# Layer 1: nearest prototypes from the products, distances on ScalarE, and an fp32 bias product

## The chip, the cores and the metric

One core of one Trainium2 chip runs the whole program in one launch. The metric is the device time of a run in microseconds (us). TensorE (PE) multiplies, VectorE (DVE), ScalarE (ACT) and GpSimd (POOL) do the elementwise work, SyncE (SP) issues most of the DMAs.

## The reference

Two layers, each a cross attention and an FFN, each added to x through a tanh gate, over 64 batches of 256 tokens of 256 values. Layer 0's FFN is a mixture of experts over the first 1024 tokens. The change lies in layer 1's FFN:

```python
def _L1_ffn_ref(x, prototypes, B, A, bias, temp):
    x2 = jnp.sum(xf * xf, axis=1, keepdims=True)
    p2 = jnp.sum(prototypes * prototypes, axis=1)
    d2 = x2 + p2[None, :] - 2.0 * (xf @ prototypes.T)
    dists = jnp.sqrt(jnp.maximum(d2, 0.0))
    t = jnp.maximum(jnp.abs(temp), 0.1)
    w = jax.nn.softmax(-dists / t, axis=1)
    topw, topi = jax.lax.top_k(w, 2)
    topw = topw / jnp.sum(topw, axis=1, keepdims=True)
    ...
        h = jnp.einsum('nri,ni->nr', B[idx], xf)
        y = jnp.einsum('nor,nr->no', A[idx], h) + bias[idx]
        out = out + wt * y
```

There are 32 prototypes with factors of rank 16, so 512 low values a token. Each token takes its two nearest prototypes. x2 is the same for all 32, so the order of the distances is that of the products 2 x p - p2.

## The kernel before

The program runs five phases one after the other: keys and values, layer 0's attention, the experts, and `attention_ffn_phase`, which holds layer 1's attention and FFN in one software pipeline over 64 batches i of two tiles (h = 0 and 1) of 128 tokens; t = 2 i + h counts tiles. Between the experts and layer 1 `Layer1Weights` splits the weights into fp16 halves.

Each engine runs its own `body(i, u, j)` in order, written out for 16 batches and looped over; the engines meet at semaphores (`need(engine, semaphore, value)` is a wait). There is no scheduler: the order on an engine is the order of the code. A body works on several tiles at once, by lag: in the body of tile t the scores of t are made, tile t-3 goes through the transposition of its probabilities (three groups, each split into `probT` hi by ScalarE, L1234, and lo by VectorE, L1492) and its output product, t-4 is normalised, t-5 gets its low products and the products with the prototypes (`dots`), t-6 its two weights, t-7 the weighing and the transposition of the selection, t-8 the up product with its bias, and the residual. In between stand the queries of the next batch, four banks of twelve products, one (the second of h=1's `prep`) at the very end of h=1.

TensorE's results go through a ring of five PSUM banks in a fixed order of uses. A bank is written only when its earlier use has been read; the second low bank of h=0 follows the first probT bank, the output bank the third. So a late `probT_lo` on VectorE stops TensorE there.

What the change touches, for tile t:

- VectorE, `prototype_products` (L1531): dots = scale times product minus |p|^2. `nearest_two` (L1540, L1544): near = min(dots - |y|^2, -tiny), then MAX8 of near. `nearest_index` (L1549): the places. A `hold` is a wait followed by a small memset.
- GpSimd, `top_weights`: dist = -top (L1179), index to float (L1180), root by a power (L1182), the difference, decay to its power (L1184), plus one (L1185). Behind it stand `weighed_low` (L1171, for which SP's transposition of hw waits) and others.
- VectorE, `pick` (L1627, twice) = (iota == index) * weight, and `wsel` (L1634) = the sum of both, written three times side by side, 96 columns. GpSimd's `weigh` (L1192) multiplies the 512 low values by it.
- TensorE transposes wsel (L1468, fp32). ScalarE evacuates 96 rows as fp16 (L1353), VectorE takes the third block's rounding off (L1608), so that wselT holds hi, hi and lo. The bias, held as hi, lo, hi, is one fp16 product over 96 rows (L1452), the last of tile t-8's bank.
- ScalarE, `length2` (L1282): |y|^2 of tile t-4, in one of two columns of `ysq`.

## Time and profile before

| | us |
|---|---|
| median of 3 runs | 3045.66 |
| lowest and highest | 3040.59, 3046.47 |
| the profiled execution | 3044.48 |
| its span, first to last instruction | 3042.80 |
| TensorE busy in it | 2739.6 (90%) |
| VectorE busy | 2507.4 (82%) |
| GpSimd busy | 2089.8 (69%) |
| ScalarE busy | 1983.7 (65%) |

Busy time counts what an engine executes; a matmul's record is longer than its share of the array, since matmuls overlap, so the distance between starts says what one costs. "h=0" and "h=1" below are the halves of a batch by TensorE's body; VectorE runs ahead, so the end of its own body of h=1 (`a_wsel`, `a_near`) falls into the stretch in which TensorE is in h=0. A line of the chain of waits is a piece of the path that ended last, followed back from the end.

### The profile page before, as it was taken

How to read it: one execution, taken by the hardware profiler on the slowest of the kernel's cores; microseconds unless marked ns; L12 is line 12 of the kernel's file. 1: busy time of each engine (PE TensorE's matmuls, PEld its weight loads, DVE VectorE, ACT ScalarE, POOL GpSimd, SP SyncE). 2: the span in 40 equal slices, each digit the busy share in tenths (PEclk: the TensorE clock that was granted, in tenths of full speed). 3: DMA queues.
4: the chain of work that ended last, by engine and by line, in shares of the span. 5: the costliest groups of instructions: out<-in, count | busy, mean ns of one | idle time of the engine just before them, and what ended most of it. 6: DMA issues, size and time to landing. Idle time of an engine off the chain costs nothing.

```text
span 3042.8 us, 96434 instructions
## 1 busy us (share of the span) xinstructions
PE 2739.6 (90%) x31534; PEld 2166.8 (71%) x31534; DVE 2507.4 (82%) x6126; ACT 1983.7 (65%) x4683; POOL 2089.8 (69%) x2777
## 2 busy tenths in 40 slices
PE   4888896899999999689699999999989999999996
PEld 2444444677777777557578888888878888888885
DVE  6877776688888888675689999899989989999885
ACT  2666666687777877575466666666656666666663
POOL 3893000567666676544388888888888888888886
PEclk9999998899999999899899999999999999999998
DMA  5987566223233232631567766666776767766663
GB/s 152 364 337 294 235 254 256 76 81 93 77 90 84 80 93 76 220 117 41 121 142 158 158 147 149 140 145 150 145 137 149 141 144 149 147 150 145 145 132 78
DMA packets 638943, 455.55 MB, mean 150 GB/s; under 512 B 389760, under 2 KB 612592, under 8 KB 633648
## 3 DMA queue, kind: packets, MB, share of 16 engines
q1 hardware_dynamic: 618288, 402.31, 52.2%
q0 software_dynamic: 7328, 23.40, 2.5%
q10 hardware_dynamic: 12960, 25.23, 2.2%
q8 instruction: 195, 3.19, 0.5%
q14 instruction: 172, 1.41, 0.2%
HBM read 235.08 MB, written 148.83 MB: 126 GB/s over the span
## 4 chain that ended last, share of the span: by engine, by line
PE 32%; DVE 6%; issue 4%; POOL 3%; SPq 2%; ACT 2%; DMA 1%; DVEq 0%; POOLq 0%; ACTq 0%
PE banks L150 10%; PE banks L152 9%; PE banks L151 9%; PE banks L1416 2%; DVE a_near L1540 2%; PE banks L1401 2%; SPq L1058 1%; DVE a_probT_lo L1492 1%; ACT a_qT_hi L1234 1%; DVE a_pick L1627 1%; DVE a_rsum L1504 1%; DVE a_wtop L1567 1%; POOL a_pn L1154 1%; DMA a_xnT<-a_xn_parts 0%; DMA a_hwT<-a_hw_parts 0%
## 5 line engine op out<-in xcount | busy, mean ns | idle before, releaser
L1234 ACT ACTIVATE a_qT_hi<-banks 128x512 f16<-128x512 f32 x252 | 150.4, 597 | 540.8 <-PE banks L152 540.8
L383 POOL TENSOR_TENSOR a_probT_lo<-a_expT,a_probT_hi 128x512 f16<-128x512 f32 x256 | 291.4, 1159 | 218.5 <-ACT a_probT_hi L466 218.5
L459 ACT ACTIVATE a_expT<-banks,a_top,w_score_scale 128x512 f32<-128x512 f32 (+1 forms) x384 | 272.4, 709 | 152.5 <-PE banks L550 146.1
L1154 POOL TENSOR_TENSOR a_pn<-a_prob,a_rsum 128x1024 f32<-128x1024 f32 (+1 forms) x256 | 310.2, 1233 | 5.8 <-DVE a_rsum L1506 5.8
L150 PE MATMUL banks<-a_xnT,w_q_hi 128*128 128x256 f16 x1024 | 281.2, 275 | 15.0 <-DMA a_xnT<-a_xn_parts 13.2
L150 PE MATMUL banks<-a_vo_front,a_probT_hi 128*128 128x256 f16 x1024 | 279.8, 273 | 9.4 <-DVE a_probT_lo L1492 6.5
L152 PE MATMUL banks<-a_xnT,w_q_lo 128*128 128x256 f16 x1024 | 280.6, 274 | 0.0
L151 PE MATMUL banks<-a_xnT,w_q_hi 128*128 128x256 f16 x1024 | 280.6, 274 | 0.0
L152 PE MATMUL banks<-a_vo_front,a_probT_lo 128*128 128x256 f16 x1024 | 279.7, 273 | 0.0
L151 PE MATMUL banks<-a_vo_front,a_probT_hi 128*128 128x256 f16 x1024 | 279.6, 273 | 0.0
L1490 DVE TENSOR_TENSOR a_qT_lo<-banks,a_qT_hi 128x512 f16<-128x512 f32 x252 | 172.0, 683 | 77.9 <-ACT a_qT_hi L1234 77.7
L1234 ACT ACTIVATE a_probT_hi<-banks 128x512 f16<-128x512 f32 (+1 forms) x384 | 197.8, 515 | 22.4 <-PE banks L1416 18.0
L1492 DVE SCALAR_TENSOR_TENSOR a_probT_lo<-banks,a_probT_hi 128x512 f16<-128x512 f32 (+1 forms) x384 | 207.2, 580 | 3.5 <-ACT a_probT_hi L1234 3.5
L550 PE MATMUL banks<-ident,a_shifted 128*128 128x128 f32 (+1 forms) x1280 | 204.2, 283 | 5.3
L2366 DVE SCALAR_TENSOR_TENSOR kv_vo_out<-banks,kv_vo_out 128x512 f16<-128x512 f32 (+1 forms) x312 | 191.4, 677 | 19.2 <-ACT kv_vo_out L2264 19.2
L1416 PE MATMUL banks<-ident,a_pn 128*128 128x128 f32 (+1 forms) x1280 | 197.3, 277 | 5.5 <-POOL a_pn L1154 3.6
L659 DVE TENSOR_TENSOR a_shifted<-banks,a_smax 128x1024 f32<-128x1024 f32 (+1 forms) x256 | 192.1, 792 | 3.8
L2264 ACT ACTIVATE kv_vo_out<-banks 128x512 f16<-128x512 f32 (+1 forms) x312 | 172.1, 602 | 30.8 <-DMA vo<-kv_vo_out 24.2
L1171 POOL TENSOR_TENSOR a_hw_parts<-a_hw,a_hw_parts 128x512 f16<-128x512 f32 x128 | 148.0, 1156 | 59.7 <-ACT a_hw_parts L1307 59.7
L649 DVE TENSOR_REDUCE a_smax<-banks 128x16 f32<-128x1232 f32 x128 | 183.5, 1434 | 2.4 <-PE banks L536 1.9
L1192 POOL TENSOR_TENSOR a_hw<-a_low,a_wsel 128x512 f32<-128x512 f32 x128 | 135.2, 1056 | 59.3 <-DVE a_wsel L1634 59.3
L1143 POOL TENSOR_TENSOR a_half<-a_prob 128x512 f32<-128x512 f32 x128 | 165.7, 1295 | 14.3 <-ACT a_prob L1324 14.3
(380 smaller groups left out, 10177.7 us busy)
## 6 DMA issues: line engine op xcount, KB each, us to landing
vo<-kv_vo_out SPq DMA_DIRECT2D x38, 2048.0 KB, 8.1
a_vo_front<-vo SPq DMA_DIRECT2D x128, 512.0 KB
kt<-kv_k_out ACTq DMA_DIRECT2D x9, 2560.0 KB, 14.9
a_k<-kt SPq DMA_DIRECT2D x64, 308.0 KB, 3.5
kv_raw_e<-in_L_ffn_w POOLq DMA_DIRECT2D x16, 1024.0 KB, 8.9
a_x<-in_x SPq DMA_DIRECT2D x64, 256.0 KB, 2.9
a_y<-in_x SPq DMA_DIRECT2D x64, 256.0 KB, 2.7
x<-a_y SPq DMA_DIRECT2D x64, 256.0 KB, 2.8
```

The lines of the kernel that those rows point to most:

```text
L150: nc.tensor.matmul(out, lhs[0], rhs[0], start=start, stop=False)
L151: nc.tensor.matmul(out, lhs[0], rhs[1], start=False, stop=False)
L152: return nc.tensor.matmul(out, lhs[1], rhs[0], start=False, stop=stop)
L383: pool.tensor_tensor(probT[b][1][:, first:end, :], expT[b][:, first:end, :], probT[b][0][:, first:end, :], ALU.subtract).then_inc(prob_rea ...
L459: act.activation(expT[1 - h][0:rows, first:end, :], bank, ACT.Exp, bias=top[0:rows, 0:1], scale=weights["score_scale"][0:rows, 0:1]).then_ ...
L550: last = nc.tensor.transpose(bank[0:rows, c * P:(c + 1) * P], shifted[1 - h][:, place:place + rows], ident[:, :])
L659: last = nc.vector.tensor_tensor(shifted[h][:, cols].rearrange("p (r h k) -> p r h k", r=TILES, k=end - first), held_scores[:, :, :, first ...
L1154: last = pool.tensor_tensor(keys_of(pn[h]), e[:, :, first:end], rsum[h][:, :].unsqueeze(2).broadcast_to([P, H, end - first]), ALU.mult)
L1234: act.activation(out, bank[:, 0:cols].rearrange("p (c s) -> p c s", c=out.shape[1]), ACT.Copy, scale=scale)\
L1416: last = nc.tensor.transpose(bank[0:rows, c * P:(c + 1) * P], pn[1 - h][:, place:place + rows], ident[:, :])
L1492: nc.vector.scalar_tensor_tensor(out=lo, in0=bank, scalar=scale, in1=hi, op0=ALU.mult, op1=ALU.subtract)\
L2366: nc.vector.scalar_tensor_tensor(out=vo_out[q][0:m, placed(b), 1, :], in0=product_banks(g, c, b, m), scalar=1.0 / OUT_TOP, in1=vo_out[q][0 ...
```

## The change

Three things. (1) The maximum and its index are sought in `dots` itself; `near` is gone, and with it the subtraction of |y|^2 before. (2) The squared distances of the two found come from ScalarE, `square_gaps`: Relu(|y|^2 - top), put in ScalarE's body one tile later, behind the first probT_hi (and, in h=1, a query bank), ahead of `norm2_log`. It waits for the maximum and is waited for by `top_weights` on GpSimd, which adds a tiny number in place of the change of sign. `ysq` has four columns. (3) The bias product runs in fp32 over 32 rows: wsel is 32 columns wide and written once, ScalarE's evacuation writes fp32, VectorE's L1608 is gone, and the bias is loaded once and only scaled.

```diff
-            for n, number in enumerate((-0.5, 0.5, -1.0, 1.0)):
+            for n, number in enumerate((-0.5, 0.5, TINY, 1.0)):
...
-    ysq = sb("ysq", [P, TPB])
-    dots, near = sb("dots", [P, NPROTO]), sb("near", [P, NPROTO])
+    ysq = sb("ysq", [P, LENGTHS])
+    dots, idle_top = sb("dots", [P, NPROTO]), sb("idle_top", [P, 1])
     top, topi, topf = sb("top", [P, 8]), sb("topi", [P, 8], U32), sb("topf", [P, 2])
-    dist, dgap, late, wtop = sb("dist", [P, 2]), sb("dgap", [P, 1]), sb("late", [P, 1]), sb("wtop", [P, 2])
+    dist, square, dgap, late, wtop = sb("dist", [P, 2]), sb("square", [P, 2]), sb("dgap", [P, 1]), sb("late", [P, 1]), sb("wtop", [P, 2])
     more, euler, decay = sb("more", [P, 1]), sb("euler", [P, 1]), sb("decay", [P, 1])
     pick = sb("pick", [P, 2, NPROTO])
-    wsel = sb("wsel", [P, P])
-    wselT = sb("wselT", [BIAS_ROWS, P], F16)
+    wsel = sb("wsel", [P, NPROTO])
+    wselT = sb("wselT", [NPROTO, P])
...
-            need(pool, top_used, t)
-            pool.tensor_tensor(dist[:, :], top[:, 0:2], numbers[:, 2:3].broadcast_to([P, 2]), ALU.mult).then_inc(top_used, 1)
+            need(pool, gap_ready, t + 1)
+            kept = pool.tensor_tensor(dist[:, :], square[:, :], numbers[:, 2:3].broadcast_to([P, 2]), ALU.add)
             pool.tensor_copy(topf[:, :], topi[:, 0:2]).then_inc(top_ready, 1)
-            need(pool, top_used, t + 1)
+            step(kept)
             step(pool.tensor_tensor(dist[:, :], dist[:, :], numbers[:, 1:2].broadcast_to([P, 2]), ALU.pow))
...
+        def square_gaps(t, h, u):
+
+            n = (TPB * u + h - 6) % LENGTHS
+            need(act, top_found, t + 1)
+            need(act, ysq_done, t + 1)
+            need(act, more_ready, t)
+            act.activation(square[:, :], top[:, 0:2], ACT.Relu, bias=ysq[:, n:n + 1], scale=-1.0).then_inc(gap_ready, 1)
...
-        def length2(t, h):
-
+        def length2(t, h, u):
+
+            n = (TPB * u + h - 4) % LENGTHS
             need(act, ln2_inverse, t + 1)
-            need(act, near_ready, t - 1)
-            act.activation(ysq[:, h:h + 1], inv2[:, :], ACT.Identity, scale=mv2[:, 1:2]).then_inc(ysq_done, 1)
+            act.activation(ysq[:, n:n + 1], inv2[:, :], ACT.Identity, scale=mv2[:, 1:2]).then_inc(ysq_done, 1)
...
                     if g == 0:
                         prep(0)
+                        if live(t - 6, NT):
+                            square_gaps(t - 6, h, u)
                         if live(t - 4, NT):
...
-                    act.activation(wselT[:, :], bank[0:BIAS_ROWS, 0:P], ACT.Copy).then_inc(wselT_hi, 1)
+                    act.activation(wselT[:, :], bank[0:NPROTO, 0:P], ACT.Copy).then_inc(wselT_ready, 1)
...
-                    filled(nc.tensor.transpose(bank[:, 0:P], wsel[:, :], ident[:, :]), i, ("wselT", h))
+                    filled(nc.tensor.transpose(bank[0:NPROTO, 0:P], wsel[:, :], ident[:, :]), i, ("wselT", h))
...
-            need(dve, near_ready, t)
+            need(dve, topi_found, t)
...
-        def nearest_two(t, h):
-
+        def nearest_two(t):
+
+            need(dve, gap_ready, t)
             need(dve, dots_read, t + 1)
-            need(dve, ysq_done, t + 1)
-            nc.vector.tensor_scalar(near[:, :], dots[:, :], ysq[:, 1 - h:2 - h], -TINY, ALU.subtract, ALU.min)\
-                .then_inc(near_ready, 1)
-            need(dve, top_used, t)
-            hold(near_ready, t + 1)
-            nc.vector.max(top[:, :], near[:, :]).then_inc(top_found, 1)
+            nc.vector.memset(idle_top[:, :], 0.0)
+            nc.vector.max(top[:, :], dots[:, :]).then_inc(top_found, 1)
 
         def nearest_index(t):
 
             hold(top_found, t + 1)
-            nc.vector.max_index(topi[:, :], top[:, :], near[:, :]).then_inc(topi_found, 1)
+            nc.vector.max_index(topi[:, :], top[:, :], dots[:, :]).then_inc(topi_found, 1)
...
-                if live(t - 7, NT):
-                    bank, rows = full(i, ("wselT", h)), slice(2 * NPROTO, BIAS_ROWS)
-                    need(dve, wselT_hi, t - 6)
-                    nc.vector.tensor_tensor(wselT[rows, :], bank[rows, 0:P], wselT[rows, :], ALU.subtract)\
-                        .then_inc(wselT_ready, 1)
...
-                    nc.vector.tensor_tensor(wsel[:, 0:BIAS_ROWS].rearrange("p (r n) -> p r n", r=3),
-                                            pick[:, 0, :].unsqueeze(1).broadcast_to([P, 3, NPROTO]),
-                                            pick[:, 1, :].unsqueeze(1).broadcast_to([P, 3, NPROTO]), ALU.add)\
-                        .then_inc(wsel_ready, 1)
+                    nc.vector.tensor_tensor(wsel[:, :], pick[:, 0, :], pick[:, 1, :], ALU.add).then_inc(wsel_ready, 1)
                 if live(t - 5, NT):
-                    nearest_two(t - 5, h)
+                    nearest_two(t - 5)
...
-        for r in range(3):
-            sp.dma_start(self.raw_bias[r * NPROTO:(r + 1) * NPROTO, :], low_bias).then_inc(self.small_in, 16)
+        sp.dma_start(self.low_bias_sb[:, :], low_bias).then_inc(self.small_in, 16)
...
-        dve, low_bias_sb, raw_bias = self.nc.vector, self.low_bias_sb, self.raw_bias
-        step = Steps(dve, self.bias_step, 0, 1)
-        step(dve.tensor_scalar(raw_bias[:, :], raw_bias[:, :], self.low_unit[0:BIAS_ROWS, 1:2], None, ALU.mult))
-        dve.tensor_copy(low_bias_sb[:, :], raw_bias[:, :]).then_inc(self.bias_hi, 1)
+        dve, low_bias_sb = self.nc.vector, self.low_bias_sb
+        dve.tensor_scalar(low_bias_sb[:, :], low_bias_sb[:, :], self.low_unit[0:NPROTO, 1:2], None, ALU.mult)
         for n, (parts, src, unit) in enumerate(self.turned_jobs):
             split16(self.nc, False, *parts, src, self.inverse[:, unit:unit + 1], self.hi_done, n + 2, self.lo_done)
-        dve.wait_ge(self.bias_hi, 1)
-        rows = slice(NPROTO, 2 * NPROTO)
-        dve.tensor_tensor(low_bias_sb[rows, :], raw_bias[rows, :], low_bias_sb[rows, :], ALU.subtract)
```

On VectorE, at the end of its body of h=1 and the start of the next body, before (a line number, the operation, out<-in):

```order
L1634 TENSOR_TENSOR a_wsel<-a_pick 128x96
L1540 TENSOR_SCALAR a_near<-a_dots,a_ysq 128x32
L847 MEMSET a_idle 128x1
L1544 MAX a_top<-a_near 128x8
L847 MEMSET a_idle 128x1
L1549 MAX_INDEX a_topi<-a_top,a_near 128x8
L62 ISA
L62 REGISTER_ALU
L1504 TENSOR_REDUCE a_rsum<-a_quarter 128x16
```

and now:

```order
L1633 TENSOR_TENSOR a_wsel<-a_pick 128x32
L1547 MEMSET a_idle_top 128x1
L1548 MAX a_top<-a_dots 128x8
L846 MEMSET a_idle 128x1
L1553 MAX_INDEX a_topi<-a_top,a_dots 128x8
L61 ISA
L61 REGISTER_ALU
L1511 TENSOR_REDUCE a_rsum<-a_quarter 128x16
```

`a_near` (L1540) is gone between `a_wsel` and the maximum; a memset of one column that waits for nothing new stands there. Behind follow, as before, the row sums and the splits that TensorE waits for.

On ScalarE, at the start of its body of h=0, behind the next batch's a_xn_parts, before:

```order
L1291 ACTIVATE a_xn_parts<-a_xn 128x2x256
L62 ISA
L1234 ACTIVATE a_probT_hi<-banks 128x512
L62 ISA
L1264 ACTIVATE a_minus_mean<-a_mv 128x1
L1265 ACTIVATE a_vare<-a_mv,eps 128x1
L1234 ACTIVATE a_probT_hi<-banks 128x512
L1324 ACTIVATE a_prob<-a_prob,w_score_scale 128x1232
```

and now:

```order
L1297 ACTIVATE a_xn_parts<-a_xn 128x2x256
L61 ISA
L1232 ACTIVATE a_probT_hi<-banks 128x512
L61 ISA
L61 REGISTER_ALU
L1276 ACTIVATE a_square<-a_top,a_ysq 128x2
L61 REGISTER_ALU
L1262 ACTIVATE a_minus_mean<-a_mv 128x1
L1263 ACTIVATE a_vare<-a_mv,eps 128x1
L1232 ACTIVATE a_probT_hi<-banks 128x512
L1332 ACTIVATE a_prob<-a_prob,w_score_scale 128x1232
```

`a_square` (L1276) has come in ahead of the statistics of the second norm; the exponential and the other pieces of `a_probT_hi` stand behind it. (ISA and REGISTER_ALU rows wait for or compute a semaphore's value.) In h=1 a query bank's `a_qT_hi` stands ahead of it too.

## Rows read from the trace of the kernel before

**Rows 1.** Busy time by engine in a batch and its second tile; TensorE's clock, DMA behind.

```profile
2157.24:2181.01 23.77, 22.53 (x278) 19.54 (x277) 21.59 (x66) 15.34 (x44) 20.62 (x30) 1.00 0.69 151
2169.13:2181.01 11.88, 10.64 (x133) 9.06 (x133) 11.46 (x36) 7.29 (x20) 10.79 (x16) 1.00 0.71 162
```

**Rows 2.** Chain of waits, batch from 2157.24: start us, length us, engine, tile, line.

```profile
2170.80 1.15 DVE a_near L1540
...
2173.93 0.28 PE banks L150
...
2174.94 0.28 PE banks L150
```

**Rows 3.** The same chain, first transposes of a batch, early and late in layer 1.

```profile
1560.21 0.44 PE banks L1416 x4
...
1823.72 0.44 PE banks L1416 x4
...
2615.38 0.44 PE banks L1416 x4
...
2898.63 0.44 PE banks L1416 x4
```

**Rows 4.** Waits of TensorE from 1500 to 2900: us in total, times, longest.

```profile
PE banks L150 <- DVE a_probT_lo L1492: 31.9, 52, 2.7
...
PE banks L150 <- DMA a_hwT<-a_hw_parts: 4.7, 8, 1.3
```

**Rows 5.** a_near: duration ns shortest/median/longest; then busy us and mean ns, all tiles.

```profile
L1540 DVE TENSOR_SCALAR a_near<-a_dots,a_ysq x128: 209/236/1141, 1526.6 to 3022.8; 128x32 f32<-128x32 f32 x128
...
L1540 DVE TENSOR_SCALAR a_near<-a_dots,a_ysq 128x32 f32<-128x32 f32 x128 | 80.3, 627 | 0.7 <-issue 0.7
```

**Rows 6.** VectorE in time, h=0 of the batch: start us, length us, operation.

```profile
2170.63 0.26 DVE L1634 TENSOR_TENSOR a_wsel<-a_pick 128x96 f32<-128x96 f32 x1
...
2172.08 0.19 DVE L1544 MAX8 a_top<-a_near 128x8 f32<-128x32 f32 x1
2172.32 0.09 DVE L1549 MATCH_VALUE_LOAD a_topi<-a_top,a_near 128x8 f32 x1
...
2173.18 1.62 DVE L1492 SCALAR_TENSOR_TENSOR a_probT_lo<-banks,a_probT_hi 128x512 f16<-128x512 f32 x3
```

**Rows 7.** GpSimd in time, the same stretch.

```profile
2169.42 0.62 POOL L1146 TENSOR_TENSOR a_quarter<-a_quarter,a_prob 128x208 f32<-128x208 f32 x1
2170.65 1.26 POOL L1161 TENSOR_TENSOR a_xn_parts<-a_xn,a_xn_parts 128x512 f16<-128x512 f32 x1 [0.61 <-ACT a_xn_parts L1291]
```

**Rows 8.** TensorE in time, the same stretch.

```profile
2170.99 0.27 PE L150 MATMUL banks<-w_upT_hi,a_hwT 128*128 128x256 f16 x1
...
2172.30 0.27 PE L1452 MATMUL banks<-w_low_bias,a_wselT 96*128 96x256 f16 x1
2172.41 0.29 PE L150 MATMUL banks<-w_downT_hi,a_ynT 128*128 128x288 f16 x1
```

**Rows 9.** TensorE in time, layer 0: fp32 products of 256 columns, and what follows.

```profile
910.17 1.03 PE L520 MATMUL banks<-a_xnT,w_qT 128*128 128x256 f32 x4
911.04 0.82 PE L550 MATMUL banks<-ident,a_shifted 128*128 128x128 f32 x6
```

**Rows 10.** ScalarE in time, the stretch of rows 6.

```profile
2170.95 0.19 ACT L1264 ACTIVATE a_minus_mean<-a_mv 128x1 f32<-128x1 f32 x1
2171.05 0.28 ACT L1265 ACTIVATE a_vare<-a_mv,eps 128x1 f32<-128x1 f32 x1
...
2173.02 0.38 ACT L1234 ACTIVATE a_probT_hi<-banks 104x256 f16<-104x256 f32 x1
```

**Rows 11.** SP's queue in time; then issue to landing of the hw transposition.

```profile
2152.61 2.06 SPq L1090 DMA_TRANSPOSE a_hwT<-a_hw_parts  x1
...
2167.28 1.28 SPq L1090 DMA_TRANSPOSE a_hwT<-a_hw_parts  x1
...
DMA to landing us min/median/max: 3.0/3.2/5.5
```

## What the change will do: the prediction

> **What bounds the kernel now.** Layer 1 with its FFN fills the second half of the span: 64 batches of two tiles, one period per batch. The first thing to read is one period as a window. From 2157.24 to 2181.01 TensorE is busy 22.53 of 23.77 us at full granted clock, no other engine over 21.6; but in the second half (TensorE's body of h=0) VectorE is busy 11.46 of 11.88 us and TensorE only 10.64 [rows 1]. In the first half TensorE is busy all the time (22.53 - 10.64 = 11.89 us). So TensorE bounds h=1, and in h=0 it waits for somebody.
>
> The chain of waits says for whom [rows 2]. When TensorE has filled the last query bank, the chain goes over ScalarE (qT_hi) to VectorE, through a_near (1.15 us for 128x32 elements!), and back to TensorE at 2173.93, where the second "low" bank needed probT_lo, and at 2174.94 for the output bank. The list of TensorE's waits agrees: 31.9 us in 52 waits on probT_lo L1492 between 1500 and 2900, against 4.7 us in 8 for the transposed hw [rows 4]. The period is not the same everywhere: 263.51 us / 11 = 23.96 early, where the expert rows are added on VectorE too, and 283.25 / 12 = 23.60 late [rows 3].
>
> Why is a_near slow? Its shortest and median times are 0.21 and 0.24 us, its longest 1.14, its mean 0.63 [rows 5]: with two levels, (0.627 - 0.236) / (1.141 - 0.236) = 43%, about one tile in two. In h=0 it starts at 2170.80, behind GpSimd's a_xn_parts of 2170.65, and ends with it (2171.91) [rows 6, 7]. The Trainium skill, SBUF — State Buffer, section "Who interferes with whom", says that VectorE's tensor_scalar in a two-port mode and GpSimd take turns on one port pair and the later one blocks wholly; the trace agrees, 0.24 us becoming 1.14.
>
> **Part 1, VectorE loses a_near.** In h=0, from the start of a_near to that of MAX8 2172.08 - 2170.80 = 1.28 us pass [rows 6]. The maximum now reads the dots, after a memset that takes some 0.03, so 1.25 go. a_wsel (0.26 us for 96 columns) shrinks to 32; that saves between nothing and two thirds of it, and I take 0.05. The next row sums and the first probT_lo start 1.3 us earlier (2173.18 to about 2171.9). The subtraction for wselT (L1608) and, in h=1, the fast a_near also go; VectorE is not late in h=1, where TensorE is never idle [rows 1], so I cost them at nothing. If h=1 had no such slack they would be worth another half microsecond.
>
> **Part 2, ScalarE gets square_gaps**, at the start of its next tile, behind the first probT_hi. Here the change adds a wait: the instruction waits for the maximum, and behind it on ScalarE stand the statistics, two probT_hi pieces and the exponential. In h=0 ScalarE comes there at 2170.95. The maximum starts at about 2170.63 + 0.17 + 0.03 = 2170.83 and is usable 0.24 later (MAX8 2172.08, its reader 2172.32), at 2171.07. So ScalarE waits 0.12 and spends a small activation's step: 0.10 is between the starts of L1264 and L1265, 0.28 is all of L1265, which like square_gaps reads a bias [rows 10]. I take 0.2. Everything behind moves by 0.32: the third probT_hi ends at 2173.02 + 0.38 + 0.32 = 2173.72. VectorE's third probT_lo is then ready for it and waiting. It takes 0.42 (three take 1.62), ends at about 2174.16, and TensorE sees it 0.14 later (2173.18 + 1.62 = 2174.80 to 2174.94): 2174.30.
>
> **Part 3, the bias product in fp32.** The trace of before has the same 256 moving columns in fp32 in layer 0: four records for two products from 910.17 to 911.04, 0.435 us a product [rows 9]. The fp16 product takes 2172.41 - 2172.30 = 0.11 [rows 8]. So it costs 0.33 us more per tile. The bound below is 0.11 more, if 32 rows of weights needed one record instead of two (I see no reason, and the row with the same columns is nearest); above it is 0.42 more, if the fp32 weights' load isn't hidden behind the 0.11 us product before it. The selection transpose and its evacuation keep their moving size: nothing.
>
> In **h=1** TensorE never waits for VectorE, so 0.33 is paid. In **h=0** it falls into the wait: TensorE comes to the first low product at 2172.41 + 0.33 = 2172.74; six products of 0.12 and six of 0.11, then the transposition of the selection 0.11, bring it to the output bank at 2174.24. That is beside 2174.30 from part 2. So h=0 ends 2174.94 - 2174.30 = 0.64 us earlier with the fp32 product already in it, and the batch gains 0.64 - 0.33 = 0.31: 23.77 becomes 23.46.
>
> The Trainium skill, FP8 and Floating Point Precision, counts true fp32 as four passes through the array; an estimate from it is 4 x 0.11 = 0.44, what the row shows.
>
> **The sum.** About 23.46 us is also TensorE's own floor in other stretches: its work per batch plus its wait for qT_lo, which the change doesn't touch. Against it, 11 early batches gain 0.50 each (5.5), about 30 middle ones 0.31 (9.3), 12 late ones 0.14 (1.7): 16.5 us. The stretches at loop ends, the fill and the drain I leave as they are: in the drain a_near and its hold go, some 0.3 us a tile, and a ScalarE step with its hand-over comes, about as much. The DMAs and small VectorE steps saved in the weights' setup are cover for nothing that shows; below 1 us.
>
> **What takes part of it back.** The transposed hw. The transposition on SP's queue starts 14.67 us after the one before it (2152.61, 2167.28), behind ten value loads, and lands after 3.2: 2170.48, where TensorE wants it at 2170.99 [rows 8, 11]. A margin of 0.5 us. The anchor of that queue is GpSimd's a_hw_parts of the batch before, so a period 0.31 shorter eats 0.31 of the margin. The wait, seen 8 times [rows 4], becomes more frequent; I take 0.1 us for each of 53 batches, 5 us. What remains is 11 to 12 us. The profiled execution took 3044.48 (span 3042.80), near the median 3045.66, so I forecast **3033 us**, 0.4% under the median.
>
> **Rivals.**
>
> *A, the queue takes all of it.* If the hw transposition is late in nearly every batch, the period settles at what SP allows. For it: the small margin. Against: only 8 waits now, and SP itself still waits for GpSimd in each batch. Then TensorE reaches the output bank about 0.3 later than computed and the gain is nothing: 3041 to 3047.
>
> *B, the block moves on to a_wsel, and it is slower.* a_wsel adds two SBUF tiles; it starts at 2170.63, GpSimd's a_xn_parts at 2170.65 [rows 6, 7]: 0.02 us decide. If GpSimd wins, a_wsel waits 1.2 us, the maximum comes as late as today, and now ScalarE stands still behind it: square_gaps at about 2172.3 instead of 2171.07, the third probT_hi 1.3 later, TensorE at about 2175.5, and 0.33 for h=1 on top. That is 0.6 + 0.3 = 0.9 a batch, 45 us over 50 batches: 3090. The point from which it decides is a_wsel's start against a_xn_parts'. Against it: GpSimd's a_xn_parts follows ScalarE's, which hangs on TensorE's last query bank (0.33 later by the fp32 product in h=1). VectorE's own steps before a_wsel are small and seem to go on when GpSimd's a_quarter ends (2169.42 + 0.62 = 2170.04), 0.6 before a_wsel; and that one hangs on h=1's ScalarE chain, later by 0.2 for square_gaps. So VectorE would win by 0.1 more than today.
> The same page of the skill (SBUF — State Buffer, same section) states that a VectorE instruction with two SBUF inputs contends with a GpSimd read: by this rule the change leaves one exposed instruction at that very place.
>
> *C, TensorE's floor is reached everywhere,* the queue keeps up and the early stretch gains its full half microsecond: 16.5 us, and some from the drain: 3024 to 3028.
>
> *D, the fp32 product is dearer*, 0.42 instead of 0.33, in both tiles: up to 0.18 x 60 = 11 us, and the gain is gone: 3044. That the fp32 product isn't paid at all, so the whole 1.0 us of waiting goes, would give 3044 - 0.9 x 55, near 2995; nothing in the trace speaks for it.
>
> **Chances.** The forecast with its own range 3028 to 3040: 0.52. A and D together, 3040 to 3048: 0.26. B, 3065 to 3095: 0.12. C: 0.10. The range 3024 to 3049 leaves out B and little else. A measurement of this kernel can tell about 0.2%, 6 us, from no change. Faster by more than that (under 3039.6): the forecast but for its upper end, and C, 0.60. Within: 0.26. Slower: B and a tail of D, 0.14.
>
> **What would show it.** In the profile after: the period 23.4 to 23.6 instead of 23.77; no slow VectorE instruction between a_wsel and the row sums; the third probT_lo waiting for ScalarE; square_gaps waiting near 0.1 us in h=0 and not in h=1; the bias product as two records of 0.22 us each from start to start. TensorE's waits on probT_lo fall from 31.9 us to under 8, those on the transposed hw rise from 4.7 to about 8. If a_wsel shows 1.2 us in most tiles h=0, B has come; if the bias product's start to start is 0.5, D; if the hw waits are over 15 us, A.

## The result, and the profile after

| | us | against before, with its 95% interval |
|---|---|---|
| before, median of 5 runs | 3043.38 | |
| changed, median of 5 runs | 3058.86 (3056.70 to 3069.08) | 1.006 (1.0044 to 1.0077) |
| the profiled execution of the changed kernel | 3063.89, span 3062.2 | |

The change makes the kernel 0.6% slower by the ratio of the runs, 15.5 us between the medians. The forecast was 3033 us, and its range ended at 3049: wrong in size and in sign.

TensorE first. One batch of the changed kernel, its chain of waits at the first transposes (middle, early, late in layer 1), and TensorE's waits between 1500 and 2900, for [rows 1], [rows 2, 3] and [rows 4]:

```profile
2113.43:2137.39 23.96, 23.42 (x281) 19.90 (x279) 19.66 (x62) 15.68 (x46) 20.44 (x30) 1.00 0.67 142
```
```profile
1581.92 0.44 PE banks L1424 x4
...
1605.99 0.44 PE banks L1424 x4
...
2113.43 0.44 PE banks L1424 x4
...
2118.29 0.62 PE banks L1460 x2
2118.91 0.23 PE banks L149
...
2137.39 0.44 PE banks L1424 x4
...
2651.12 0.44 PE banks L1424 x4
...
2675.19 0.44 PE banks L1424 x4
```
```profile
PE banks L149 <- DVE a_probT_lo L1499: 6.0, 6, 2.7
PE banks L149 <- DMA a_hwT<-a_hw_parts: 2.3, 2, 1.2
```
The waits that the change was to shorten are gone (31.9 us became 6.0), VectorE is busy 19.7 us a batch instead of 21.6, and still the batch takes 23.96 us in the middle and 24.07 early and late, where it took 23.77, 23.96 and 23.60. TensorE's own work has grown, from 22.53 to 23.42 us busy a batch. Weighted as in the prediction, 11 x 0.11 + 30 x 0.19 + 12 x 0.47 = 12.5 us.

The profiled execution is 3063.89 - 3044.48 = 19.4 us longer than that of before. Most of the rest lies in two batches of 26.92 and 28.60 us (from one a_xn_parts of ScalarE to the next; the ordinary one is 24.0), 2.9 and 4.6 more. In each TensorE waited 1.2 us for the transposed hw, and just behind that its granted clock (PEclk, the value before the DMA share) was at the lower level, 1.2 GHz, for 3.4 (from 1934) and 6.8 us (from 2327):

```profile
2326.44 0.27 PE L149 MATMUL banks<-w_upT_hi,a_hwT 128*128 128x256 f16 x1 [1.16 <-DMA a_hwT<-a_hw_parts]
```
```profile
2326.80:2333.40 6.60, 6.60 (x29) 3.97 (x27) 5.00 (x13) 3.48 (x12) 6.37 (x12) 0.50 0.83 190
```
With work at half speed for so long, 1.2 + 1.7 = 2.9 and 1.2 + 3.4 = 4.6 account for both. The profiled execution of before has one such batch (29.53 us, clock down at 2222), and the changed kernel has that one too (29.59). No trace tells how often this happened in the other executions, so the last 3 of the 15.5 us between the medians stay unassigned.

The place is the bias product. TensorE's products, then its weight loads, in h=0 (start us, length us; brackets: idle before):

```profile
2128.99 0.27 PE L151 MATMUL banks<-w_upT_hi,a_hwT 128*128 128x256 f16 x1
2129.19 0.69 PE L1460 MATMUL banks<-w_low_bias,a_wselT 32*128 32x256 f32 x2
2129.82 0.30 PE L149 MATMUL banks<-w_downT_hi,a_ynT 128*128 128x288 f16 x1
```
```profile
2128.88 0.10 PEld L151 LDWEIGHTS banks<-w_upT_hi,a_hwT 128*128 128x128 f16 x1
2129.19 0.29 PEld L1460 LDWEIGHTS banks<-w_low_bias,a_wselT 32*128 32x128 f32 x2 [0.21 <-issue]
2129.81 0.10 PEld L149 LDWEIGHTS banks<-w_downT_hi,a_ynT 128*128 128x128 f16 x1 [0.33 <-issue]
```
The last up product of before, for the same step:

```profile
2172.19 0.27 PE L152 MATMUL banks<-w_upT_hi,a_hwT 128*128 128x256 f16 x1
```
From the start of the last up product (L151) to the first down product (L149) 0.83 us pass; before it was 0.22 (2172.19 to 2172.41 [rows 8]). That is 0.61 more a tile, not 0.33; the medians over the 111 and 112 bias products between 1560 and 2900 are the same 0.83 and 0.22. And each ordinary load starts one product early (L151's at 2128.88, its product at 2128.99), while the 32-row load and the one behind it start together with their own products.

VectorE and GpSimd in the same half, for [rows 6, 7]:

```profile
2127.19 0.19 DVE L1633 TENSOR_TENSOR a_wsel<-a_pick 128x32 f32<-128x32 f32 x1
2127.30 0.19 DVE L1548 MAX8 a_top<-a_dots 128x8 f32<-128x32 f32 x1
...
2130.41 0.42 DVE L1499 SCALAR_TENSOR_TENSOR a_probT_lo<-banks,a_probT_hi 104x256 f16<-104x256 f32 x1 [0.71 <-ACT a_probT_hi L1232]
```
```profile
2127.46 1.16 POOL L1159 TENSOR_TENSOR a_xn_parts<-a_xn,a_xn_parts 128x512 f16<-128x512 f32 x1 [1.05 <-ACT a_xn_parts L1297]
```
Nothing is blocked, a_wsel starts 0.27 ahead of GpSimd (0.02 before), and the third probT_lo waits for ScalarE, all as foretold. (Over all batches from 1560 to 2900, one a_wsel of 55 in h=0 took over 0.9 us.)

### The profile page after: what moved, and what is told of

The parts are those of the page before. It is cut to its first block, busy times and chain, and to the rows that moved or that the text cites. A ratio compares the mean times of both kernels' runs of the same rounds, so it can differ in the third digit from the quotient of the medians.

```text
span 3062.2 us, 96399 instructions
## 1 busy us (share of the span) xinstructions
PE 2802.6 (92%) x31662; PEld 2190.9 (72%) x31662; DVE 2394.4 (78%) x5868; ACT 2007.3 (66%) x4811; POOL 2085.3 (68%) x2776
## 3 DMA queue, kind: packets, MB, share of 16 engines
q0 software_dynamic: 7328, 23.40, 2.5%
## 4 chain that ended last, share of the span: by engine, by line
PE 45%; issue 2%; ACT 2%; DVE 1%; SPq 1%; DMA 1%; POOL 1%; POOLq 0%; DVEq 0%; ACTq 0%
PE banks L149 12%; PE banks L151 11%; PE banks L150 11%; PE banks L1409 4%; PE banks L1424 4%; PE banks L1460 2%; DVE a_qT_lo L1497 1%; ACT a_qT_hi L1232 1%; DMA a_hwT<-a_hw_parts 1%; SPq L1057 0%; PE banks L1476 0%; ACT a_prob L1332 0%; DMA a_xnT<-a_xn_parts 0%; ACT a_probT_hi L1232 0%; ACT a_xn L839 0%
## 5 line engine op out<-in xcount | busy, mean ns | idle before, releaser
L149 PE MATMUL banks<-a_xnT,w_q_hi 128*128 128x256 f16 x1024 | 281.3, 275 | 12.6 <-DMA a_xnT<-a_xn_parts 11.5
L149 PE MATMUL banks<-a_vo_front,a_probT_hi 128*128 128x256 f16 x1024 | 279.3, 273 | 8.4 <-DVE a_probT_lo L1499 8.3
L151 PE MATMUL banks<-a_xnT,w_q_lo 128*128 128x256 f16 x1024 | 280.9, 274 | 0.0
L151 PE MATMUL banks<-a_vo_front,a_probT_lo 128*128 128x256 f16 x1024 | 279.2, 273 | 0.0
L1499 DVE SCALAR_TENSOR_TENSOR a_probT_lo<-banks,a_probT_hi 128x512 f16<-128x512 f32 (+1 forms) x384 | 214.2, 583 | 50.1 <-ACT a_probT_hi L1232 47.9
L1232 ACT ACTIVATE a_probT_hi<-banks 128x512 f16<-128x512 f32 (+1 forms) x384 | 196.7, 512 | 16.6 <-PE banks L1424 14.1
```

Source lines behind the costliest of these rows:

```text
L149: nc.tensor.matmul(out, lhs[0], rhs[0], start=start, stop=False)
L151: return nc.tensor.matmul(out, lhs[1], rhs[0], start=False, stop=stop)
L1232: act.activation(out, bank[:, 0:cols].rearrange("p (c s) -> p c s", c=out.shape[1]), ACT.Copy, scale=scale)\
L1499: nc.vector.scalar_tensor_tensor(out=lo, in0=bank, scalar=scale, in1=hi, op0=ALU.mult, op1=ALU.subtract)\
```

## The experiments

Two theories stood against each other at first. **Rows**: TensorE pays for a product whose weights have few rows. **Block or stall**: something in parts 1 and 2 holds VectorE or ScalarE up. A ratio below is to runs of the kernel before on the same chip, with its 95% interval; the medians of before were 3042 to 3050 us there, so ratios can be compared from one experiment to another, and times only roughly. Each diff shows the lines of an edit that matter, and "..." stands for the others.

### e1_half_bias: parts 1 and 2 alone

Part 3 taken back:
```diff
-                    filled(nc.tensor.transpose(bank[0:NPROTO, 0:P], wsel[:, :], ident[:, :]), i, ("wselT", h))
+                    filled(nc.tensor.transpose(bank[:, 0:P], wsel[:, :], ident[:, :]), i, ("wselT", h))
...
+                    nc.vector.tensor_tensor(wsel[:, 0:BIAS_ROWS].rearrange("p (r n) -> p r n", r=3),
...
```


> Parts 1 and 2 alone: maximum in the dots, square_gaps on ScalarE, with the old fp16 bias product over 96 rows (hi, lo, hi). My theory: the changed kernel is late because its fp32 bias product takes 0.72 us of TensorE instead of 0.11, not because of parts 1 and 2. Then this kernel has a period of 23.77 - 0.64 = 23.1 us (output bank of h=0 reached by ScalarE's third probT_hi, 2174.30 in the terms of the prediction) and, over about 53 batches, a time 25 to 34 us under before: 3010 to 3020. Rival: the SP queue with the transposed hw limits the period to 23.3 to 23.5: 3022 to 3032. Second rival: ScalarE's added step, with its wait, eats part 1: no faster than before, 3040 or more.

Measured: 3068.08 us, ratio 1.0092 (1.0075 to 1.0109); a batch takes 24.27 us. VectorE, GpSimd, ScalarE in h=0, and ScalarE's waits:

```profile
2153.97 1.18 DVE L1642 TENSOR_TENSOR a_wsel<-a_pick 128x96 f32<-128x96 f32 x1
```
```profile
2153.88 1.15 POOL L1162 TENSOR_TENSOR a_xn_parts<-a_xn,a_xn_parts 128x512 f16<-128x512 f32 x1 [0.50 <-ACT a_xn_parts L1300]
```
```profile
2155.38 0.30 ACT L1279 ACTIVATE a_square<-a_top,a_ysq 128x2 f32<-128x2 f32 x1 [1.09 <-DVE a_top L1552]
```
```profile
ACT a_square L1279 <- DVE a_top L1552: 58.6, 55, 1.5
```
This is the mechanism of rival B: GpSimd starts 0.09 us before a_wsel, a_wsel takes 1.18 instead of 0.26, and ScalarE stands still for the maximum 55 times. In the changed kernel it hardly happens; why is taken up behind e10. The Trainium skill, SBUF — State Buffer, section "Who interferes with whom", states that a VectorE instruction with two SBUF inputs contends with a GpSimd instruction that reads SBUF; this trace agrees, 0.26 us becoming 1.18.

### e2_bias_alone: part 3 alone on the kernel before

```diff
-    wselT = sb("wselT", [BIAS_ROWS, P], F16)
+    wselT = sb("wselT", [NPROTO, P])
```


> Part 3 alone on the kernel before: the fp32 bias product over 32 rows, near and its subtraction kept. If the fp32 product costs 0.61 us more per tile: h=1 pays 0.61; in h=0 VectorE reaches the output bank at 2174.94 as before while TensorE comes at about 2173.91 + 0.61 = 2174.5, so nothing is paid there. Period 23.77 + 0.6 = 24.4, over 53 batches +32 us: 3070 to 3080. If the product cost 0.33 as predicted: +0.33, 3058 to 3064. If it were slower only beside square_gaps: 3043 to 3050.

Measured: 3062.19 us, ratio 1.008 (1.0064 to 1.0097), a batch 24.07 to 24.13 us, TensorE's waits on probT_lo 5.0 us. Part 3 alone costs what the whole change costs (0.8% and 0.6%, the intervals overlap). The time falls into the range that was given for a price of 0.33, but not for that reason: the product's price is 0.83 - 0.22 = 0.61 here too. What failed is the assumption that VectorE's chain stays in h=0. a_near is still there, and none of its 55 instances in h=0 between 1560 and 2900 took over 0.9 us, against 51 of 56 before:

```profile
L1537 DVE TENSOR_SCALAR a_near<-a_dots,a_ysq 128x32 f32<-128x32 f32 x114 | 28.3, 248 | 0.7 <-issue 0.7
```

### e3_rows128: the changed kernel, its product padded with zeros to 128 rows

```diff
-    wsel = sb("wsel", [P, NPROTO])
-    wselT = sb("wselT", [NPROTO, P])
+    wsel = sb("wsel", [P, P])
+    wselT = sb("wselT", [P, P])
...
-        self.low_bias_sb = sb("low_bias", [NPROTO, D])
+        self.low_bias_sb = sb("low_bias", [P, D])
```


> The changed kernel with the bias product still in fp32, but over all 128 rows: the selection and the bias are padded with zeros (96 rows of nothing), so TensorE, ScalarE's evacuation and the weight load have 128 rows. Theory rows (a product over 32 rows among products over 128 breaks TensorE's overlap at both ends): the product falls from 0.72 to the 0.435 us of layer 0, period 23.96 to about 23.4 to 23.5, time 3028 to 3038. Theory type (fp32 behind fp16 breaks it, whatever the rows): 0.65 to 0.75 us stays, 3055 to 3065.

Measured: 3033.63 us, ratio 0.9975 (0.9966 to 0.9985). One batch, products, loads:

```profile
2129.61:2153.01 23.40, 22.86 (x281) 20.03 (x279) 19.49 (x62) 15.74 (x46) 20.46 (x30) 1.00 0.69 148
```
```profile
2144.88 0.27 PE L151 MATMUL banks<-w_upT_hi,a_hwT 128*128 128x256 f16 x1
2144.99 0.60 PE L1462 MATMUL banks<-w_low_bias,a_wselT 128*128 128x256 f32 x2
2145.42 0.29 PE L149 MATMUL banks<-w_downT_hi,a_ynT 128*128 128x288 f16 x1
```
```profile
2144.88 0.30 PEld L1462 LDWEIGHTS banks<-w_low_bias,a_wselT 128*128 128x128 f32 x2
2145.21 0.10 PEld L149 LDWEIGHTS banks<-w_downT_hi,a_ynT 128*128 128x128 f16 x1
```
Four times the rows, and 25 us less. The product takes 0.43 us, loads run ahead again, and a batch is 0.56 shorter; twice 0.83 - 0.54 = 0.29 makes 0.58. The rows, not fp32 as such, are what went wrong.

### e4_half_rows32: 32 rows in fp16

The low parts of weights and bias are left out here, so it computes less exactly; it shows only the rows' price in the cheap type.
```diff
-    wselT = sb("wselT", [NPROTO, P])
+    wselT = sb("wselT", [NPROTO, P], F16)
```


> The changed kernel with the bias product over 32 rows, but in fp16 of one part: selection and bias are rounded to fp16 and their low parts are left out. Theory rows: the product still has a gap ahead of it and behind it, 0.2 to 0.4 us in all against 0.11, period 23.2 to 23.5. Theory type: 0.11 us, no gap, period about 23.1, as in the kernel with parts 1 and 2 alone.

Measured: 3030.3 us, ratio 0.996 (0.9945 to 0.9976).

```profile
2148.57 0.27 PE L151 MATMUL banks<-w_upT_hi,a_hwT 128*128 128x256 f16 x1
2148.78 0.28 PE L1460 MATMUL banks<-w_low_bias,a_wselT 32*128 32x256 f16 x1
2148.99 0.30 PE L149 MATMUL banks<-w_downT_hi,a_ynT 128*128 128x288 f16 x1
```
0.42 us from L151 to L149 instead of 0.22 for the 96-row product: 0.10 ahead and 0.10 behind, without any fp32. So the price of 32 rows is 0.20 in fp16 and 0.83 - 0.54 = 0.29 in fp32. The single records of the fp32 product say where it loses 0.10 more than the fp16 one: over all bias products of the changed kernel the first record starts 0.20 behind L151, the second 0.32 behind the first, L149 0.31 behind the second; in e3 it is 0.11, 0.22 and 0.22. So about 0.10 is lost at each of three starts, one of them between two records of 32 rows each.

### e8_rows64: 64 rows, the transposition as in e3

```diff
-    wselT = sb("wselT", [P, P])
+    wselT = sb("wselT", [2 * NPROTO, P])
...
-        self.low_bias_sb = sb("low_bias", [P, D])
+        self.low_bias_sb = sb("low_bias", [2 * NPROTO, D])
```


> e3_rows128 (the fp32 bias product padded with zeros) with 64 rows instead of 128 in the product, the transposition ahead of it as in e3 over the full 128 columns. Theory rows, by degrees (every product with fewer rows than its neighbours breaks the overlap): 0.6 to 0.72 us for the product, period 23.8 to 24.1, time 3050 to 3062. Theory only 32 rows (96 rows in fp16 cost 0.11 with no gap, so the break starts below 64): 0.44 us, period 23.4, time 3030 to 3038. A third: what cost in the changed kernel was the 32-row transposition and not the product; then this run has 0.44 us too and the gap is to be sought behind the transposition.

Measured: 3065.59 us, ratio 1.0061 (1.004 to 1.0081), a batch 23.97 us.

```profile
2146.72 0.27 PE L151 MATMUL banks<-w_upT_hi,a_hwT 128*128 128x256 f16 x1
2146.93 0.70 PE L1462 MATMUL banks<-w_low_bias,a_wselT 64*128 64x256 f32 x2
2147.56 0.30 PE L149 MATMUL banks<-w_downT_hi,a_ynT 128*128 128x288 f16 x1
```
Again 0.84 from L151 to L149, no better than 32 rows; and the transposition is cleared, since it was the full one. With 96 rows (fp16, [rows 8]) and 128 there is no gap, with 32 and 64 there is: a step, not a slope. Few columns of weights do nothing of the kind. The transposition of the selection in the changed kernel has 128 rows and 32 columns, and the product behind it starts 0.10 later:

```profile
2131.22 0.27 PE L1476 MATMUL banks<-ident,a_wsel 128*32 128x128 f32 x1
2131.32 0.27 PE L149 MATMUL banks<-a_vo_front,a_probT_hi 128*128 128x256 f16 x1
```
A rule of the Trainium skill that I hadn't weighed bears on this: TensorEngine Tiling (Array Packing), section "Tiling Modes", has 32 and 64 rows as modes of their own beside the full array, and states "Mode switching requires drain". The gaps ahead of and behind the product agree with it. The gap between the two fp32 records, where the rows don't change, is not explained by it, and the same section has 128 rows by 32 columns as a mode too, where this trace shows no gap. So the step between 64 and 96 rows is measured (with 96 rows tried in fp16 alone), and its mechanism stays open.

The kernel before already had such a step. Its attention scores (L1401) are fp16 products with 64 rows. Four fp32 transpositions ahead of full-height products take 0.43 us to the next start, ahead of the scores 0.54, and the first load of the scores starts with its own product:

```profile
2157.08 0.60 PE L1416 MATMUL banks<-ident,a_pn 128*128 128x128 f32 x4
2157.51 0.27 PE L150 MATMUL banks<-a_xnT,w_q_hi 128*128 128x256 f16 x1
...
2158.82 0.60 PE L1416 MATMUL banks<-ident,a_pn 128*128 128x128 f32 x4
2159.36 0.25 PE L1401 MATMUL banks<-a_k,a_qT_hi 64*128 64x77 f16 x4
```
```profile
2159.35 0.12 PEld L1401 LDWEIGHTS banks<-a_k,a_qT_hi 64*128 64x128 f16 x4 [0.17 <-issue]
```

### e5_bias_first: the 32-row product at the front of its bank

```diff
+                    nc.tensor.matmul(bank[:, 0:D], wselT[:, :], ffn["bias"][:, :], start=True, stop=False)
...
-                    filled(nc.tensor.matmul(bank[:, 0:D], wselT[:, :], ffn["bias"][:, :], start=False, stop=True),
```


> The changed kernel with the 32-row fp32 bias product moved from the end of its bank to the front: it opens the sum, right behind two fp32 transpositions, and the four chunks of three fp16 products follow. Theory position (the cost comes from a short weight load that has to stand between fp16 products of 128 rows, and the fp32 transpositions ahead already leave a gap): one of the two gaps goes, the product costs 0.4 to 0.5 us, period about 23.6, time 3035 to 3045. Theory rows (whatever stands around it, the load of the 32-row block and the load behind it are not overlapped): product still 0.65 to 0.75 us, period 23.95 to 24.1, time 3055 to 3065. One more: TensorE then waits for wselT with the bank's first product instead of its last; wselT is ready well before, so this should cost nothing.

Measured: 3069.33 us, ratio 1.0078 (1.0052 to 1.0103), a batch 23.96 us. In the chain of waits:

```profile
2122.02 0.62 PE banks L1457 x2
2122.64 0.22 PE banks L149
```
0.62 + 0.22, as in the changed kernel (0.62 + 0.23). Where it stands doesn't matter, as theory rows had it.

### e9_rows128_alone: part 3 alone, padded to 128 rows

e2_bias_alone with the padding of e3_rows128, so `near` and the old distances are there.
```diff
-    wselT = sb("wselT", [NPROTO, P])
+    wselT = sb("wselT", [P, P])
```


> The kernel before with part 3 alone, and its fp32 bias product padded with zeros to 128 rows (e3_rows128 without parts 1 and 2). Theory of the prediction (with the product at 0.44 us TensorE's work is about 23.4 to 23.5 a batch, under the 23.77 that VectorE's chain sets in the kernel before; that chain is shortened only by what part 3 takes off VectorE): period 23.6 to 23.8, time 3035 to 3050, and so parts 1 and 2 are worth the 5 to 15 us between this run and e3_rows128. Rival (parts 1 and 2 bring nothing; what e3_rows128 gained comes from part 3 taking a subtraction and 64 columns off VectorE): time 3028 to 3036, period 23.4, like e3_rows128.

Measured: 3033.98 us, ratio 0.9949 (0.9934 to 0.9965), the gain of e3 without parts 1 and 2. a_near over 1500 to 2900, and its place in h=0:

```profile
L1539 DVE TENSOR_SCALAR a_near<-a_dots,a_ysq 128x32 f32<-128x32 f32 x116 | 28.8, 249 | 0.4 <-issue 0.4
```
```profile
2097.21 0.19 DVE L1628 TENSOR_TENSOR a_wsel<-a_pick 128x32 f32<-128x32 f32 x1
2097.32 0.23 DVE L1539 TENSOR_SCALAR a_near<-a_dots,a_ysq 128x32 f32<-128x32 f32 x1
```
```profile
2097.56 1.16 POOL L1160 TENSOR_TENSOR a_xn_parts<-a_xn,a_xn_parts 128x512 f16<-128x512 f32 x1 [1.03 <-ACT a_xn_parts L1290]
```
a_near takes 0.25 us in the mean instead of 0.63 [rows 5]. Nobody removed it: VectorE now passes ahead of GpSimd.

### e11 and e12: both padded kernels side by side

> e3_rows128 once more (all three parts, the product padded to 128 rows), on the same chip and against the same runs of before as e12: the two came from different series, at 3033.6 and 3034.0 us. Theory of the prediction (parts 1 and 2 shorten VectorE's chain, and that chain still sets part of the time): 3 to 10 us under e12. Rival (TensorE's work sets the period in both, so parts 1 and 2 are worth nothing there): within 3 us of e12.

> e9_rows128_alone once more (part 3 alone, its product padded to 128 rows), beside e11. Theory of the prediction: 3036 to 3045 where e11 has 3033. Rival: 3031 to 3036, the same as e11 within 3 us, since the subtraction and the extra columns that part 3 takes off VectorE are enough to let a_near start ahead of a_xn_parts.

Measured: with parts 1 and 2 3032.86 us (0.9958, 0.9945 to 0.9971), without them 3035.95 (0.997, 0.9959 to 0.998). The intervals overlap, and by its ratios the first pair of runs (e3 0.9975, e9 0.9949, on two chips) had the opposite order. If parts 1 and 2 are worth anything beside the padded product, it is less than these runs can tell.

### e6, e7 and e10: can the fp16 product be kept?

Three attempts to have parts 1 and 2 with the 0.11 us product. e6: e1_half_bias with ScalarE's square behind its third split.
```diff
-                        if live(t - 6, NT):
-                            square_gaps(t - 6, h, u)
...
+                if live(t - 6, NT):
+                    square_gaps(t - 6, h, u)
```


> e1_half_bias (parts 1 and 2 with the fp16 product) with ScalarE's square of the two gaps issued behind its third split of the probabilities instead of behind its first: whatever holds up VectorE's maxima then holds up no split. Theory stall (the 55 waits of ScalarE for a_top, 58.6 us in 1400, are what the blocked a_wsel costs): they go, TensorE's waits for probT_lo fall from 54.8 us to under 30, period 23.5 to 23.8, time 3030 to 3045. Theory VectorE's own path (the 1.2 us that a_wsel is blocked is itself on the chain, since the third a_probT_lo comes behind it): the waits of ScalarE go but the period stays 24.1 to 24.3 and the time 3060 to 3070.

e7: e1_half_bias with GpSimd's `weigh` ahead of `rows_low`.
```diff
-                if h == 0 and live(i + 1, NB):
-                    rows_low(i + 1)
                 if live(t - 7, NT):
                     weigh(t - 7, 1 - h)
+                if h == 0 and live(i + 1, NB):
+                    rows_low(i + 1)
```


> e1_half_bias with two rows of GpSimd's order swapped in h = 0: the product that weighs low by a_wsel first, a_xn_parts' low parts behind it. GpSimd then can't start a_xn_parts before a_wsel is written, so the 1.2 us for which a_wsel is blocked can't happen. Theory block (rival B of the prediction is what e1 paid): a_wsel back to 0.26 us in every tile, period 23.0 to 23.3, time 3000 to 3020, faster than before. Theory phases (the order of parts 1 and 2 with 96 columns is slower for another reason): a_wsel is short but the period stays above 23.8. Theory given back (GpSimd's low parts end 1.2 us later and something else is blocked by them: the maxima, the matching or the third a_probT_lo): another VectorE row shows 1 us or more in half the tiles, period 23.5 to 24.0, time 3030 to 3055.

e10: the changed kernel with 96 fp16 rows stacked behind the transposition.
```diff
-                    act.activation(wselT[:, :], bank[0:NPROTO, 0:P], ACT.Copy).then_inc(wselT_ready, 1)
+                    act.activation(wselT[0:NPROTO, :], bank[0:NPROTO, 0:P], ACT.Copy).then_inc(wselT_hi, 1)
+                    act.activation(wselT[2 * NPROTO:BIAS_ROWS, :], bank[0:NPROTO, 0:P], ACT.Copy).then_inc(wselT_two, 1)
...
+                    nc.vector.tensor_tensor(wselT[NPROTO:2 * NPROTO, :], bank[0:NPROTO, 0:P], wselT[0:NPROTO, :], ALU.subtract)\
...
```


> The changed kernel with the fp16 bias product of 96 rows again, but its weights stacked behind the transposition and not ahead of it: a_wsel stays 32 columns wide, ScalarE copies the 32 transposed rows twice (rows 0 to 31 and 64 to 95), VectorE writes the low half to rows 32 to 63. The product should cost 0.11 us as in the kernel before, with the transposition of 32 columns as in the changed kernel. Theory TensorE's floor: 0.33 us a tile less than e3_rows128 on TensorE, so that VectorE's chain or a wait for transposed data sets the period at 23.1 to 23.4, time 3012 to 3032, the fastest of all. Rival block (as in e1_half_bias: it is the phase of GpSimd against VectorE, not the width of a_wsel, that decides, and the added subtraction on VectorE brings back the old phase): a_wsel is blocked for 1 us or more in about half the tiles, period 24.0 to 24.3, time 3055 to 3068. Rival queue: ScalarE's second copy (0.2 us) delays its last split of q, period 23.4 to 23.7, time 3030 to 3045.

Measured: e6 3064.81 us (1.0048, 1.0036 to 1.0061), e7 3048.57 (0.9999, 0.9987 to 1.0011), e10 3071.6 (1.0076, 1.0062 to 1.0089). The waits of e6 (one of GpSimd, one of TensorE), then of e7 (TensorE), then a_wsel in e10:

```profile
POOL a_dist L1180 <- ACT a_square L1279: 120.6, 112, 2.8
...
PE banks L150 <- DMA a_hwT<-a_hw_parts: 16.6, 17, 2.7
```
```profile
PE banks L150 <- DVE a_probT_lo L1503: 23.4, 48, 2.7
...
PE banks L150 <- DMA a_hwT<-a_hw_parts: 14.1, 12, 1.8
PE banks L150 <- DMA a_xnT<-a_xn_parts: 9.4, 15, 1.1
```
```profile
L1641 DVE TENSOR_TENSOR a_wsel<-a_pick 128x32 f32<-128x32 f32 x112 | 68.6, 612 | 3.8
```
e6 takes ScalarE's stall away, and TensorE's waits for probT_lo fall from 54.8 to 20.8 us; but GpSimd now waits for the square in nearly every tile (in e1 2.2 us in 8 waits) and feeds TensorE and the queue later. About half of e1's loss goes (ratio 1.0048, e1 1.0092). e7 takes the block away (no a_wsel over 0.9 us), and with it the whole loss against before, yet it gains nothing: TensorE waits 14.1 + 9.4 + 3.3 = 26.8 us for transposed data, of which the first is rival A's hw, and still 23.4 us for probT_lo. The 3000 to 3020 us that theory block gave were missed. e10 shows that width isn't what decides: a_wsel of 32 columns is blocked too (mean 0.61 us).

One measure orders these kernels: by how much GpSimd's a_xn_parts starts behind a_wsel in h=0 (median of all batches between 1560 and 2900, 54 to 56 a kernel). Beside it stands the product's step, from L151 to L149.

| kernel | step of the product, us | GpSimd behind a_wsel, us | over 0.9 us |
|---|---|---|---|
| e10_half_stacked | 0.22 | -0.16 | a_wsel, in 54 of 54 |
| e1_half_bias | 0.22 | -0.15 | a_wsel, in 54 of 54 |
| before | 0.22 | +0.03 | a_near, in 51 of 56 |
| e4_half_rows32 | 0.42 | +0.04 | a_wsel, in 2 of 56 |
| e3_rows128 | 0.54 | +0.17 | none |
| e9_rows128_alone | 0.54 | +0.27 | none |
| changed | 0.83 | +0.27 | a_wsel, in 1 of 55 |

e4, e3 and the changed kernel differ in the bias product and its padding alone, and the lead grows with the product's price. GpSimd's a_xn_parts starts 0.71 us behind ScalarE's in every one of these kernels, while a_wsel starts 0.87 (e10), 0.66 (e4), 0.54 (e3) and 0.44 us (changed) behind it. So it is ScalarE and GpSimd together that become later against VectorE. Parts 1 and 2 pull the other way, by 0.1 to 0.2 us (e1 against before, e3 against e9). That the shift comes over TensorE's last query bank, which a dearer product in h=1 delays, fits all rows and is not shown by a run of its own. Between e10 and e4 the subtraction on VectorE goes too, so that step has two candidates.

## Why the prediction was wrong

**The step that failed is the price of part 3**: "So it costs 0.33 us more per tile", with bounds of 0.11 and 0.42. It measured 0.61. Twice 0.28 more over 53 batches is 30 us, which turns the 12 us of gain into 18 us of loss; 15.5 were measured. The row it came from [rows 9] was of the same type and the same moving columns but had 128 rows of weights, and I wrote of 32 rows only that they might be cheaper. With 128 rows the price was right to 0.01 (0.54 - 0.22 = 0.32 in e3). My upper bound, one load not hidden, counted one gap of about 0.10; the runs show three, ahead of the product, between its two records and behind it. The trace of before had a nearer row than the one I took, the way into the 64-row scores, with one such gap in it.

**Its effect on the sum.** TensorE's floor in the prediction was 23.46 us with twice 0.33 in it, so 22.80 without. With twice 0.61 it is 24.02, and 23.96 to 24.07 was measured. The floor passed the old period, so in h=0, where "it falls into the wait", the cover was used up too.

**Part 1 and part 2 themselves.** a_near gone, nothing blocked behind it, third probT_lo waiting for ScalarE (0.71), waits on probT_lo 6.0 us: as foretold, though e2 shows that with part 3 alone these waits fall to 5.0 us too. ScalarE's square waits 4 times in all between 1500 and 2900 (0.12 in each h=0 was forecast), since MAX8 starts 0.11 behind a_wsel, not 0.20, and a_wsel itself comes 0.24 sooner against ScalarE's a_xn_parts (0.44 behind it, before 0.68). With the product at the forecast price the batch took 23.40 us and the kernel 3033.6, against 23.46 and 3033: part of that is luck. For **the cause of the gain was mis-assigned**: e9 and e12 reach it without parts 1 and 2, and e1, which has them alone, is 0.9% slower. In the prediction part 3 was only a cost, and the 0.33 by which it delays GpSimd's a_xn_parts appeared only in rival B, as a reason why a_wsel would not be blocked. In the kernel before, a_near started 0.15 us behind GpSimd. With part 3 it starts 0.06 sooner behind a_wsel (0.11 instead of 0.17), and the lead of a_wsel over GpSimd grows by 0.24 (0.03 to 0.27): the narrower a_wsel alone would not have freed it, the shift of the lead does.

**The rivals.** D (dearer product) was what came, priced at 0.42 and so bounded by 3044; B came in e1 and e10 and cost 26 and 22 us. The prediction had 45, but with 0.3 a batch for the fp32 product, which these two don't have; without it the forecast is 0.6 a batch, 30 us, and 0.50 was measured (24.27 against 23.77), so B was priced about rightly; A came in e7, and not in the changed kernel, whose hw waits fell to 2.3 us. Of the chance of slower, 0.14, 0.12 was B, and only 0.02 was left for a product so dear that the kernel gets slower, which came.

## What to carry to other kernels

A matmul's price is that of its neighbourhood: here weights of 32 or 64 rows between full ones cost 0.2 (fp16) to 0.3 us (fp32) over a product of 96 or 128 rows. So pad with zeros where the weights can be kept padded, and take prices only from rows of the same height. Where GpSimd can block VectorE, note the lead of one over the other at the critical place in hundredths of a microsecond; an edit on a third engine that moves either of them can decide more than the instructions it removes. The fastest full version here is the changed kernel padded to 128 rows, or part 3 alone so padded, at 0.25 to 0.5% under before.

## What the runs showed of the hardware

- A 32- or 64-row product among 128-row ones: loads are not taken ahead at either end (idle 0.21 and 0.33 us of the load side in the changed kernel). 32 rows cost 0.20 us more than 96 in fp16 (e4), 0.29 more than 128 in fp32; 64 rows cost the same in fp32 (e8). A load itself is no slower (0.10 us for 128 rows, 0.09 for 32 in e4), as the Trainium skill, TensorE: Matmul & The Clock Gate, section "LDWEIGHTS (loading the stationary operand)", has it.
- A product of 128 rows and 32 columns among full ones has no such gap (0.10 to 0.11 us to the next start in the changed kernel).
- An fp32 product with 128 rows and 256 moving columns takes 0.43 us behind fp16 products (e3), and its loads of two records run ahead of it.
- An add of two SBUF tiles on VectorE is held by GpSimd in either width: 0.26 to 1.18 us for 96 columns (e1), 0.19 to 1.14 for 32 (e10). It was held in all 54 batches of e1, in which it starts 0.06 to 0.17 us behind GpSimd's instruction, and in 2 of 56 of e4: the two in which it starts behind (by 0.08 and 0.15 us), while the others are ahead, by 0.04 in the median.
- A granted clock of 0.50, the 1.2 GHz level, for 6.8 us behind a wait of 1.16 us made one batch 28.60 us instead of 24.0 (changed kernel, at 2326).
